# A transformer block on one core: batch 0's opening rebuilt, stores on two queues, and the order planned with other due times

## What is computed

```python
x = x + _L0_attn_ref(_layernorm(x, axis=-1), L0_attn_W_attn, L0_attn_W_proj)
x = x + _L0_ffn_ref(_layernorm(x, axis=-1), ...)
```

```python
K = _get_slice(k_cum, l_idx, r_idx)
mask = t[:, None] >= r_idx[None, :]
att_logits = jnp.einsum('bhtd,bhsd->bhts', q, K) * scale
...
logits = jnp.concatenate([att_logits, att_tail[..., None]], axis=-1)
att = jax.nn.softmax(logits, axis=-1)
```

## Time and profile before

| | |
|---|---|
| Time, median of 3 runs | 650.69 us (650.59 to 652.74) |
| The profiled execution | 650.5 us |
| Its span, first to last instruction | 648.4 us |
| PE busy | 560.4 us, 86% |
| VectorE, ScalarE, GpSimd busy | 380.3, 380.4, 282.1 us |
| Mean granted clock of TensorE | 0.93 of full speed |

### The profile page before, as it was taken

The page is one execution under the profiler, slowest core; times in us unless marked ns, Lnnn a source line. Parts: engine busy times, 40 slices in busy tenths (PEclk is TensorE's granted clock), DMA queues, the critical chain, the costliest instruction groups (busy, mean ns, idle before and its releaser), DMA issues.

```text
span 648.4 us, 10506 instructions
## 1 busy us (share of the span) xinstructions
PE 560.4 (86%) x3568; PEld 271.1 (42%) x3568; DVE 380.3 (59%) x935; ACT 380.4 (59%) x543; POOL 282.1 (44%) x403
## 2 busy tenths in 40 slices
PE   1434778888897999889999979999998999999997
PEld 1132123243343435345445334544445434566553
DVE  2626876966878583677756991765767703605400
ACT  1310136674654686467675568677666698675764
POOL 2400303702622573335535662436436424565675
PEclk9755579898997998979999989999999999999999
DMA  6484000184320208605214049334205222234352
GB/s 154 132 210 86 1 3 3 45 208 129 83 68 25 79 4 226 178 35 129 75 50 136 31 126 211 104 85 105 75 27 162 71 67 82 85 114 144 102 175 87
DMA packets 49337, 63.45 MB, mean 98 GB/s; under 512 B 8484, under 2 KB 30788, under 8 KB 48004
## 3 DMA queue, kind: packets, MB, share of 16 engines
q1 hardware_dynamic: 49284, 62.78, 35.7%
HBM read 50.31 MB, written 12.06 MB: 96 GB/s over the span
## 4 chain that ended last, share of the span: by engine, by line
PE 58%; DVE 17%; SPq 9%; DMA 6%; issue 4%; ACT 3%; POOL 2%; POOLq 0%; DVEq 0%; ACTq 0%
PE sums_ps L1060 16%; PE ring L1048 13%; PE sums_ps L992 9%; DVE MXR L1162 6%; SPq L598 6%; PE ring L975 4%; PE ring L953 3%; DMA XP<-in_x_dram 3%; PE ring L913 2%; PE ring L970 2%; PE ring L999 2%; PE ring L1027 2%; PE ring L947 2%; DMA WB<-combine 2%; DMA QA<-MB 1%
## 5 line engine op out<-in xcount | busy, mean ns | idle before, releaser
L727 POOL TENSOR_TENSOR H<-RV,WB 128x512 f32<-128x512 f32 x128 | 164.2, 1295 | 164.5 <-ACT RV L830 130.1
L819 ACT ACTIVATE PT<-ring 128x1024 f32<-128x1024 f32 x160 | 158.5, 1022 | 96.5 <-PE ring L975 95.8
L1162 DVE TENSOR_REDUCE MXR<-ring 128x4 f32<-128x1024 f32 (+2 forms) x192 | 176.0, 952 | 61.3 <-PE ring L953 58.3
L1060 PE MATMUL sums_ps<-H,wdown 128*128 128x512 f32 x288 | 149.4, 616 | 1.4 <-POOL H L727 1.1
L877 ACT ACTIVATE RV<-ring 128x512 f32<-128x512 f32 x144 | 85.5, 594 | 74.8 <-PE ring L1048 72.8
L992 PE MATMUL sums_ps<-PT,VA 128*32 128x512 f32 (+1 forms) x768 | 91.7, 560 | 0.0
L1048 PE MATMUL ring<-XH,WUH 128*128 128x512 f32 x144 | 80.8, 561 | 2.4 <-DVE MB L1273 1.7
L830 ACT ACTIVATE RV<-RV 128x512 f32<-128x512 f32 x128 | 80.6, 630 | 3.7
L975 PE MATMUL ring<-QA,KA 54*128 54x512 bf16 (+1 forms) x384 | 61.7, 359 | 8.3 <-DMA QA<-MB 5.0
L1060 PEld LDWEIGHTS sums_ps<-H,wdown 128*128 128x128 f32 x288 | 48.8, 189 | 38.1 <-issue 25.3
L953 PE MATMUL ring<-KA,QA 51*128 51x256 bf16 (+7 forms) x512 | 61.9, 308 | 0.0
(11 more groups left out here) (128 smaller groups left out, 660.6 us busy)
## 6 DMA issues: line engine op xcount, KB each, us to landing
WB<-combine SPq DMA_DIRECT2D x256, 128.0 KB, 2.9
QA<-q_parts SPq DMA_DIRECT2D x16, 384.0 KB, 6.3
q_parts<-Qparts SPq DMA_DIRECT2D x16, 192.0 KB, 3.9
KA<-k_parts SPq DMA_DIRECT2D x8, 384.0 KB, 5.7
XP<-in_x_dram SPq DMA_DIRECT2D x4, 512.0 KB, 6.1
X<-in_x_dram SPq DMA_DIRECT2D x4, 512.0 KB, 4.9
q_parts<-Qparts SPq DMA_DIRECT2D x16, 128.0 KB, 3.6
out_dram<-OT SPq DMA_DIRECT2D x8, 256.0 KB, 2.4
```

Of the source, the lines that this page charges most:

```text
L727: pool.tensor_tensor(H[:, m % NHB, :], RV[:, m % NRV, :], WB[:, r % NWB, :], ALU.mult).then_inc(s_had, 1)
L819: act.activation(dst, src, ACT.Exp, scale=SCALE).then_inc(s_expa, 1)
L1060: pe.matmul(dsum, wdown[:, CHUNKS[n], :], H[:, m % NHB, :], start=(n == 0), stop=(n == NCH - 1)).then_inc(s_dn, 1)
L1162: ins = dve.reduce_max(MXR[:, g, i, :, q0:q0 + nq], pair("max", b, w, g, n)[:, :, at:at + ns * nq].rearrange("p e (q s) -> p e q s", s=ns) ...
```

## The change

In batch 0 and ahead of it:

- ScalarE runs one exponential of a single column first, before it waits for anything else of the program.
- PE runs 30 matmuls of zeros with zeros (128 x 128, f32) into the bank `ring` 0 ahead of its first real work.
- Of the six stores of K and of each window of Q in batch 0, SP issues the three of the even half, ScalarE the three of the odd half. All still count on the same semaphores.

For all batches, the planner's numbers differ: the lags from a load to what uses it (4.5 to 5.0, 1.2 to 1.5 for the rows), STAY, and all due times. `whigh` and `wlow` get a due time of their own, 25.0.

```diff
-            put(("kst", b), "sp", 3.9, ("ksplit", b, 1), later(old("kld", b - 1), 4.5))
+            put(("kst", b), "sp", 3.9 if b else 2.0, ("ksplit", b, 1), later(old("kld", b - 1), 5.0))
+            if b == 0:
+                put(("kst_odd", b), "act", 2.0, ("ksplit", b, 1))
...
-SWITCH, STAY = 0.09, 4.9
-STARTUP, PERIOD = 40.0, 103.4
+SWITCH, STAY = 0.09, 23.5
+STARTUP, PERIOD = 40.0, 105.8
...
+        def store_pieces(eng, dst, parts, pieces, signal, halves):
+
+            for a, js in enumerate(pieces):
+                for e in halves:
+                    to = dst[e, js].rearrange("j d q s -> (d q) j s")
+                    _, n, size = to.shape
+                    eng.dma_start(to, parts[HALF * e:HALF * e + HALF, a].unsqueeze(1).to_broadcast([HALF, n, size])).then_inc(signal, 16)
...
-                store_pieces(Kd, Kparts, K_PIECES, s_kd)
+                store_pieces(sp, Kd, Kparts, K_PIECES, s_kd, (0, 1) if b else (0,))
...
+            act.wait_ge(s_init, 2)
+            act.activation(first[:, :], zeros[:, 0:1], ACT.Exp)
             act.wait_ge(s_init, 7)
...
+                elif kind == "kst_odd":
+                    act.wait_ge(s_ksplit, 1)
+                    store_pieces(act, Kd, Kparts, K_PIECES, s_kd, (1,))
...
+            pe.wait_ge(s_init, 2)
+            for _ in range(WARM):
+                pe.matmul(ring[:, 0, 0:P], zeros[:, 0:P], zeros[:, 0:P], start=True, stop=True)
             pe.wait_ge(s_w, 16 * N_FIRST)
```

More of the change, by code:

```diff
@@ L98 @@
 PIECES = len(PART_PAIRS)
+WARM = 30
 def unit_of(r):
@@ L155, in work @@
         for h in range(2):
-            put(("stats1", b, h), "dve", 0.8, (("xload", b), 3.5))
+            put(("stats1", b, h), "dve", 0.8, (("xload", b), 5.0 if b else 3.5))
         put(("aggr1", b), "dve", 0.85, ("stats1", b, 1))
@@ L177, in work @@
         put(("prod", b), "dve", 1.17, ("evac", b, "v"), ("tails", b, 0), ("qsplit", b, 1, 1))
-        put(("kst", b), "sp", 3.9, ("ksplit", b, 1), later(old("kld", b - 1), 4.5))
-        put(("kld", b), "sp", 0.7, (("kst", b), 1.9), old2("expa", b - 2, 1, NG - 1, len(EXP_UNITS[1]) - 1))
+        put(("kst", b), "sp", 3.9 if b else 2.0, ("ksplit", b, 1), later(old("kld", b - 1), 5.0))
+        if b == 0:
+            put(("kst_odd", b), "act", 2.0, ("ksplit", b, 1))
+        put(("kld", b), "sp", 0.7, (("kst", b), 1.9), None if b else (("kst_odd", b), 1.9), old2("expa", b - 2, 1, NG - 1, len(EXP_UNITS[1]) - 1))
         for w in range(NW):
-            put(("qst", b, w), "sp", 3.9, ("qsplit", b, w, 1), later(old("qld", b - 1, w), 4.5))
-            put(("qld", b, w), "sp", 0.7, (("qst", b, w), 1.9), old("expa", b - 1, w, NG - 1, len(EXP_UNITS[w]) - 1))
+            put(("qst", b, w), "sp", 3.9 if b else 2.0, ("qsplit", b, w, 1), later(old("qld", b - 1, w), 5.0))
+            if b == 0:
+                put(("qst_odd", b, w), "act", 2.0, ("qsplit", b, w, 1))
+            put(("qld", b, w), "sp", 0.7, (("qst", b, w), 1.9), None if b else (("qst_odd", b, w), 1.9), old("expa", b - 1, w, NG - 1, len(EXP_UNITS[w]) - 1))
         put(("xres", b), "sp", 0.45, old("x1", b - 1, 1))
@@ L201, in work @@
                     back = pv_number(b, w, g, step_of_exp(w, n)) - NPT
-                    put(("exp", b, w, g, n), "pe", 0.23 + (0.11 * nh // 2 if c // 2 == w else 0), (("rows", b, w, g), 1.2),
+                    put(("exp", b, w, g, n), "pe", 0.23 + (0.11 * nh // 2 if c // 2 == w else 0), (("rows", b, w, g), 1.5),
                         ("pv", back // PVN) + PVS[back % PVN] if back >= 0 else ("wlow", 0))
@@ L259 @@
 ROWS_OF = {"max": 64, "exp": 64, "pv": 32}
-SWITCH, STAY = 0.09, 4.9
-STARTUP, PERIOD = 40.0, 103.4
[L262 to L265, removed]
+SWITCH, STAY = 0.09, 23.5
+STARTUP, PERIOD = 40.0, 105.8
+OFF = {"att0": -41.6, "att1": 48.0, "ffn0": 100.9, "ffn1": 157.9, "prep": -54.0, "post": -5.4, "max": -48.4}
+UNIT_T = 3.2
+AHEAD = {"pe": 0, "act": 0.06, "dve": 0.04, "pool": 0.14, "sp": 0.54}
+SHIFT = {"kld": -9.0, "relu": -5.9, "sq": 13.4, "up": -4.0, "aT": -11.1, "tails": 28.0, "split": 5.4, "evac": -29.1, "qst": 6.7, "oevac": 6.4, "max": -0.1, "mT": -15.2, "pv": 8.4, "dn": 21.3, "had": 6.3, "red": -10.8, "fill": -11.4, "mfin": 9.9, "rows": -3.5, "ocopy": -17.8, "exp": -7.5, "oT": 14.8}
 ATTEND = ("max", "red", "mfin", "split", "mT", "mcopy", "rows", "exp", "expa", "pv", "oevac", "oT", "ocopy", "td", "et", "tailw")
@@ L269 @@
 PREP = ("xload", "stats1", "aggr1", "rstd1", "apply1", "fill", "evac", "tails", "sums", "ksplit", "qsplit", "prod", "kst", "kld", "qst",
-        "qld", "xres", "whigh", "wlow")
+        "qld", "xres", "whigh", "wlow", "kst_odd", "qst_odd")
 def due(name):
@@ L281, in stage_due @@
     at = STARTUP + PERIOD * b
+    if kind in ("whigh", "wlow"):
+        return 25.0
     if kind in PREP:
@@ L426, in build @@
         zeros = sb("zeros", [P, WT * NE])
+        first = sb("first", [P, 1])
         XN = sb("XN", [P, NT, C])
@@ L590, in constants @@
                 sp.dma_start(wdown[:, :, :], down.rearrange("(k p) c -> p k c", p=P)).then_inc(s_w2, 16)
[L592 to L598, removed]
             def store_k(b):
@@ L618, in store_q @@
                     sp.wait_ge(s_qa[w], 32 * b)
-                store_pieces(Qd[w], Qparts[:, :, window(w)], Q_PIECES, s_qd[w])
+                store_pieces(sp, Qd[w], Qparts[:, :, window(w)], Q_PIECES, s_qd[w], (0, 1) if b else (0,))
             def load_q(b, w):
@@ L837, in _ @@
                     exponent(b, *k)
+                elif kind == "kst_odd":
+                    act.wait_ge(s_ksplit, 1)
+                    store_pieces(act, Kd, Kparts, K_PIECES, s_kd, (1,))
+                elif kind == "qst_odd":
+                    w = k[0]
+                    act.wait_ge(s_qsplit, w + 1)
+                    store_pieces(act, Qd[w], Qparts[:, :, window(w)], Q_PIECES, s_qd[w], (1,))
                 elif kind == "oevac":
```

6 lines of the change are left out of this document (3 added, 3 removed).

## The result

The changed kernel takes 626.81 us (median of 4, 626.08 to 630.03) where the kernel before takes 650.86 (4 runs): ratio 0.9634, 95% interval 0.9596 to 0.9672. That is 24 us, where 9.7 were forecast, outside the range. In two later comparisons the ratio was 0.9578 (0.9524 to 0.9633) and 0.9581 (0.9544 to 0.9618). Medians here are over all executions of a comparison; ratios leave out those in a slower state, 3 of the changed kernel's 16, which also had a lower clock.

What follows compares the result with a forecast made beforehand. PE bounds the kernel from about 200 us on; in the opening PE waits on one chain. From 650.5 us, 4.9 for the opening and 4.7 for fewer row-group changes give 640.9, so 641; range 634.5 to 647.5.

Steps and rivals of the forecast that it cites:

- the term for PE's waits under the new due times: PE's gaps between 200 and 600 us: no change taken, with 4 us either way.
- PE waits there anyway: The 19 fewer row-group changes before 200 us: costed at nothing because PE waits there; 1.9 us if not.
- the gaps after 200 us shrink as well: Rival, chance 0.13: PE's 7.75 us idle between 200 and 300 us loses half, giving 637 us or less.
- Row groups: PE after 200 us: 47 fewer row-group changes at 0.10 us each save 4.7 us.
- The regrouping wins nothing: Rival, chance 0.18: PE's saved changes become waits for ScalarE or VectorE; only the opening counts, 645.8 us.
- The opening: Start of the program, up to the first exp: gives 4.9 us, between 3.2 and 6.5.
- Table load: Activation table load after the transposes: leaves the path whole, 1.28 us, since the dummy exponential runs during x's load.
- Warm-up: Zeros ahead of transposes and K projection: end near 9.5 us and save 2.0 of a possible 2.7 us.
- the clock is back down before K: Rival, chance 0.10: lower clock returns before the K projection, 2.0 us less gained, 643 us.
- Two queues: Batch 0's K and q stores, 0.66 us issue each on both queues: 3.1 us from shorter issue, none in transport.
- The order behind the opening: VectorE's first maxima copy behind six reductions, not three: first exp gains 3.2 of 6.5 us, part regained later.
- The rows' chain exposed: Rival, chance 0.07, slower: delayed maxima expose the chain to exp in 32 groups; at 0.5 us each, 656.9 us.

Runs made afterwards that it cites:

- opening only: Kernel before with the changed kernel's opening and the old orders on every engine: 649.11 us, ratio 0.9927 to the kernel before.
- orders only: Changed kernel's orders with the old opening (no zeros, no early exponential, SP issuing all stores): 628.13 us, ratio 0.9606; again 629.21, ratio 0.9626.
- Experiment 5: Kernel before with 64 more matmuls of zeros ahead of nine units that PE waits for, 100 to 520 us: 652.66 us, ratio 0.9976.
- experiment 4: Changed kernel with batch 1's first-window q load and maxima rows moved ahead of six q stores on SP: 626.59 us, beside the changed kernel's 625.53.
- short stay: Changed kernel with STAY back at 4.9 and the new due times, 382 row-group changes: 637.28 us, ratio 0.9746 to the kernel before.
- experiment 2: Changed kernel with STAY back at 4.9: 637.28 us, ratio 0.9746; kernel before with STAY at 23.5 and old due times: 655.91 us, ratio 1.0022.

## Why the prediction was wrong, by its steps

**The failing step** is the term for PE's waits under the new due times, which the sum put at nothing. The prediction says "I take no change" of the gaps between 200 and 600, and has no term at all for the stretch from 100 to 200 us, where it notes only that "PE waits there anyway". The due times were read as a means to fewer changes; they are also what sets PE's waits. What was said of 200 to 600 us held: there the idle time is the same within about 1 us. Of the 9.0 us of idle time that went, 5.7 went between 100 and 200 us. The rival that comes nearest, "the gaps after 200 us shrink as well", 0.13, looked in the wrong stretch: between 200 and 300 us 7.75 became 7.65.

**A term left out** is the clock behind the opening. The earlier trace rows showed 0.92 between 200 and 300 us, and the sum took nothing from it. In the traces it is 9.3 us, part of it chance. By the mean clock of all executions compared, the lower clock holds 90 us in the kernel before (0.931 of 44), 91 with the opening only (0.929 of 7), 80 in the changed kernel (0.936 of 16) and 73 with orders only (0.9415 of 10). The orders thus take 11 to 17 us off it, at most 6 to 8 us of PE's time. Over the 16 executions of the changed kernel the span grows by 0.38 us with each microsecond more at the lower clock, over the 44 of the kernel before by 0.22. That such a microsecond costs this much is an estimate from executions that differ by themselves; by it the 11 to 17 us are worth 2 to 6 us.

Whether the clock follows from the waits is only in part shown. The rows of the table with over 87 us idle have 12.8 or more, but those under 83 have anything from 2.3 to 13.4. The Trainium skill, TensorE: Matmul & The Clock Gate, section HAM oscillation — how this bites in real kernels, ties a clock that falls in mid-kernel to TensorE's waits for DMA. Experiment 5 agrees (mean clock 0.942 beside 0.931 with the waits filled), with two reserves from experiment 4: the wait there was for VectorE and not for a DMA, and behind the same wait the clock doesn't always fall.

**Row groups**, mechanism as predicted, size a little small. Work falls by 6.4 us for 66 changes, 0.10 each as read from the earlier trace rows; the sum had costed the 19 ahead of 200 us at nothing. But the short stay's 9 to 12 us for 60 changes show that the term of work holds more than these changes. And the changes alone do not reach the end: 54 fewer with old due times, no gain (experiment 2). "The regrouping wins nothing", with 0.18, is what happens without new due times.

**The opening**, 4.9 forecast, 4.8 measured alone. That these agree is partly luck, for steps inside were off, and in the trace with the opening only the x transposes of batch 1 are 3.1 us ahead (100.77 against 103.90). Table load gone, right. Warm-up: zeros over at 9.5, right to the tenth. The clock's part was 2.3 us in six traces of eight (transposes 0.9, K projection 3.43 to 2.00 in the chain), 1.0 in the first trace, where the rival "the clock is back down before K" is seen; 2.0 was fair. The four records of batch 1 that the prediction took for its K projection (1.72) are the V projection; K there takes 1.92, which fits the 2.00. Two queues: wrong in size. Three K stores take 2.93 and 2.41 us, 0.8 to 1.0 each where one queue alone takes 0.66, and the K load goes out at 31.8, not 30.0. The six q stores of a queue take 6.01 and 5.41 and end at 38.7, not 35.0. The chain of the changed kernel has the transport of the stores between them, start us, us, what:

```profile
28.62 3.17 DMA k_parts<-Kparts
...
34.36 6.29 DMA q_parts<-Qparts
...
41.55 7.79 DMA XP<-in_x_dram
```

x goes out at 41.55 in place of 37.95, 3.6 late; its landing takes 7.79 (I had 9.95 with the contention), so the maxima start 1.5 late. The changed kernel's later execution has its K projection 1.3 us sooner and issues that load only 0.4 earlier (41.15). The Trainium skill, DMA: Bandwidth & Descriptors, section Issuing engines are not separate DMA queues, says that two issuing engines save only the sequencer's time; the trace agrees, and shows less than that saved: 1.0 of 3.94 us for the K stores, where issue at the old price on both queues would have saved 2.0.

**The order behind the opening**: right that the first exp gains less than the maxima (1.2 us against 5.0). **The tail**: unchanged, as forecast; from the last window's first proj to the end 65 us both times (583.45 and 559.68 to the end). **The rows' chain exposed**, the slower rival, did not come as a whole; one such wait stands at 140 us, 3.69 us long, where the kernel before has one of 2.65 at 144.

**What stays open**: which single due time removes which wait. The two tables only fit each other, and neither alone explains it. Then how much of the gain is the clock, and whether the shorter waits brought it. And how much of the opening's 4.8 us is left in the new order: between nothing and 3.

## What to carry to other kernels

When a change touches the numbers that order a program, count PE's idle time and its time at the lower clock as terms of their own, with bounds as wide as half of what the trace shows, over the whole span and not only where PE looks full; a constant's named effect (fewer row-group changes) may be only a part of what it moves, and may need the other constants to show at all. Tables found by one search belong together: swapping one back lost two thirds of the gain. And compare several executions before explaining 5 us: here three traces of one program spread over 10 us, 8.5 of them in the clock term.

## What the runs showed of the hardware

- One program's profiled spans lay at 620.8, 625.0 and 630.9 us, and near-identical ones at 616.2 to 631.0; much of the difference goes with the lower clock's price, 2.9 to 14.7 us.
- With two queues issuing at once each store's issue is longer: 0.8 to 1.0 us in place of 0.66.
- Behind one and the same wait for VectorE (3.40 and 3.28 us) the clock stayed at 1.00 in one execution and fell to 0.51 in another.
- Zeros bring the transposes from 1.94 to 1.06 us, and in six traces of eight the clock holds for the K projection, across two idle stretches of 1.0 to 2.0 and 1.2 us; in the other two (2.1 and 0.8, then 1.2 us) it did not.
